# Row gathers of a DLRM tower: each waits for the one before to land, and POOL's program is written out block by block

## What is computed

```
e = stack([tbl_f[ids[:, f]] for f in range(26)], axis=1)      # 2048 x 26 x 64
x = layer_norm(dense @ Wd.T)                                   # 128 values
y = layer_norm(einsum('bnd,ed->bne', e, Ws))
y = layer_norm(einsum('bne,pn->bep', y, Wsi))                  # 32 vectors of 128
T = concatenate([x, y]);  Z = T @ T.T;  z = layer_norm(tril(Z) @ Wl.T) * mask
h = relu([z, dense] @ W1 + b1);  h = relu(h @ W2 + b2);  out = h @ W3
```

## Time and profile before

| | us |
|---|---|
| median of 3 runs | 1114.89 |
| lowest and highest run | 1108.34, 1116.1 |
| span of the profiled execution | 1104.1 |
| of it PE busy | 727.6 |
| of it DVE busy | 468.6 |
| of it POOL busy | 406.8 |
| of it ACT busy | 374.8 |

### The profile page before, as it was taken

The page is one execution under the profiler, slowest core; times in us unless marked ns, Lnnn a source line. Parts: engine busy times, 40 slices in busy tenths (PEclk is TensorE's granted clock), DMA queues, the critical chain, the costliest instruction groups (busy, mean ns, idle before and its releaser), DMA issues.

```text
span 1104.1 us, 18935 instructions
## 1 busy us (share of the span) xinstructions
PE 727.6 (66%) x7419; PEld 555.6 (50%) x7419; DVE 468.6 (42%) x777; ACT 374.8 (34%) x1024; POOL 406.8 (37%) x454
## 2 busy tenths in 40 slices
PE   2226556676666776666786675876666866669977
PEld 1114344454444565545565554564444655448866
DVE  4314245554343445324354342445323454337851
ACT  0022324333332244223243332334323244226742
POOL 6744444424344432344432344423344332440000
PEclk9867666878677877777878777888668877789999
DMA  7300001011101101020110201101110010101110
GB/s 236 110 18 17 15 17 32 14 34 27 29 17 27 31 23 27 13 42 17 27 27 10 40 17 34 23 11 38 24 33 17 13 38 20 33 16 18 28 19 1
DMA packets 30751, 33.94 MB, mean 31 GB/s; under 512 B 10056, under 2 KB 23120, under 8 KB 30288
## 3 DMA queue, kind: packets, MB, share of 16 engines
q1 hardware_dynamic: 17344, 19.08, 7.5%
q0 software_dynamic: 13312, 13.66, 6.4%
q10 hardware_dynamic: 16, 0.01, 0.0%
HBM read 25.37 MB, written 0.01 MB: 23 GB/s over the span
## 4 chain that ended last, share of the span: by engine, by line
another core or an unknown queue 38%; PE 33%; ACT 11%; issue 9%; DVE 7%; SPq 1%; DMA 1%; ACTq 0%; DVEq 0%
PE bank_u L372 13%; ACT emb L704 4%; ACT sq L600 3%; PE bank_g L359 2%; PE bank_t L349 2%; PE bank_z L396 2%; PE bank_y L383 1%; PE bank_m L434 1%; PE bank_y L384 1%; PE bank_y L385 1%; PE bank_h L407 1%; PE bank_m L436 1%; PE bank_m L435 1%; PE bank_h L409 1%
## 5 line engine op out<-in xcount | busy, mean ns | idle before, releaser
L265 POOL DMA_INDIRECT emb<-in_tables,idx x416 | 399.2, 960 | 128.6 <-issue 128.6
L372 PE MATMUL bank_u<-mix_w,emb 128*64 128x192 f32 (+4 forms) x1024 | 159.9, 365 | 70.2 <-ACT emb L704 63.6
L905 DVE RECIPROCAL srs<-sstd 128x32 f32<-128x32 f32 x64 | 22.3, 349 | 427.7 <-ACT sstd L604 387.4
L372 PEld LDWEIGHTS bank_u<-mix_w,emb 128*64 128x64 f32 x1024 | 123.1, 171 | 105.5 <-ACT emb L704 68.4
L247 POOL COPY idx<-ids 128x13 int32 (+1 forms) x33 | 7.3, 222 | 451.5 <-PE bank_u L372 448.1
L589 ACT COPY zc<-bank_z 128x272 f32<-128x272 f32 x64 | 24.4, 381 | 426.7 <-remote 406.0
L396 PE MATMUL bank_z<-tt 128*32 128x34 f32 x4096 | 87.1, 203 | 73.3 <-issue 68.7
L349 PE MATMUL bank_t<-eye,emb 128*128 128x128 f32 x224 | 46.4, 323 | 113.2 <-ACT xb L676 57.2
L396 PEld LDWEIGHTS bank_z<-tt 128*32 128x32 f32 x4096 | 62.4, 112 | 94.9 <-issue 84.6
L704 ACT ACTIVATE emb<-emb,rstd 128x64 f32<-128x64 f32 x416 | 106.3, 339 | 0.0
L359 PE MATMUL bank_g<-gram_w,embt 128*128 128x128 f32 (+1 forms) x448 | 74.7, 314 | 42.7 <-issue 38.3
(11 more groups left out here) (133 smaller groups left out, 1152.5 us busy)
## 6 DMA issues: line engine op xcount, KB each, us to landing
emb<-in_tables,idx POOLq DMA_INDIRECT x416
zs<-zc SPq DMA_DIRECT2D x64, 70.0 KB, 2.4
zs<-zc SPq DMA_DIRECT2D x64, 42.0 KB, 2.1
wfull<-in_wfull SPq DMA_DIRECT2D x1, 2048.0 KB
dtx<-in_dense_pos SPq DMA_DIRECT2D x8, 256.0 KB
dt_f<-in_dense SPq DMA_DIRECT2D x8, 256.0 KB
wz_f<-in_wrows SPq DMA_DIRECT2D x1, 1792.0 KB
wfull<-in_w SPq DMA_DIRECT2D x1, 1280.0 KB
```

The source lines that it names most:

```text
L265: pool.indirect_dma_start(emb[:, k, D * t:D * t + D], None, x_in["tables"], bass.IndirectOffsetOnAxis(ap=idx[:, k, t:t + 1], axis=0),).the ...
L372: mm = pe.matmul(bank_u[D * a:D * a + D, o:o + PR * cnt], emb[:, k, D * t:D * t + D], mix_w[:, t, :, :].rearrange("p s v -> p (s v)")[:, w ...
```

## The change

POOL no longer uses `over_supers`. Its 32 blocks are written out with constants (`gather(n)` for n from 0 to 31). The waits ahead of a block are the same. In front of each gather but the very first there is a new wait: for the landing of the gather before it, by the semaphore on which that one counts (`first_in[k]` for tiles 1 to 8, `rows_in[k]` for tiles 9 to 12, and `rows_in` of the block before for tile 0). Nothing on the other engines changes.

```diff
-            def body(i, blocks, supers):
-                for k in range(4):
-                    n = 4 * i + k
-                    if not blocks(n):
-                        continue
-                    after(pool, mixed, 2 * n - 6)
-                    if blocks(n - 3):
-                        before = i if k < 3 else i + 1
-                        pool.wait_ge(first_in[(k + 1) % 4], 16 * FIRST * before)
-                        pool.wait_ge(rows_in[(k + 1) % 4], 16 * (TILES - FIRST) * before)
-                    pool.wait_ge(idx_ok, n + 1)
-                    if blocks(n + 1):
-                        copy_indices(n + 1, (k + 1) % 4)
-                    for t in range(TILES):
-                        pool.indirect_dma_start(
...
+            def gather(n):
+                k, before = n % 4, (n - 3) // 4 + 1
+                after(pool, mixed, 2 * n - 6)
+                if n >= 3:
+                    pool.wait_ge(first_in[(k + 1) % 4], 16 * FIRST * before)
+                    pool.wait_ge(rows_in[(k + 1) % 4], 16 * (TILES - FIRST) * before)
+                pool.wait_ge(idx_ok, n + 1)
+                if n + 1 < NBLK:
+                    copy_indices(n + 1, (k + 1) % 4)
+                for t in range(TILES):
+                    if 0 < t <= FIRST:
+                        pool.wait_ge(first_in[k], 16 * (FIRST * (n // 4) + t))
+                    elif t:
+                        pool.wait_ge(rows_in[k], 16 * ((TILES - FIRST) * (n // 4) + t - FIRST))
+                    elif n:
+                        pool.wait_ge(rows_in[(k - 1) % 4], 16 * (TILES - FIRST) * ((n - 1) // 4 + 1))
+                    pool.indirect_dma_start(
...
-            over_supers(pool, body)
+            for n in range(NBLK):
+                gather(n)
```

More of the change, by code:

```diff
@@ L247, in copy_indices @@
                 pool.tensor_copy(idx[:, k, :], ids[:, bass.ds(TILES * n, TILES)]).then_inc(idx_ok, 1)
-            def body(i, blocks, supers):
-                for k in range(4):
-                    n = 4 * i + k
-                    if not blocks(n):
-                        continue
-                    after(pool, mixed, 2 * n - 6)
-                    if blocks(n - 3):
-                        before = i if k < 3 else i + 1
-                        pool.wait_ge(first_in[(k + 1) % 4], 16 * FIRST * before)
-                        pool.wait_ge(rows_in[(k + 1) % 4], 16 * (TILES - FIRST) * before)
-                    pool.wait_ge(idx_ok, n + 1)
-                    if blocks(n + 1):
-                        copy_indices(n + 1, (k + 1) % 4)
-                    for t in range(TILES):
-                        pool.indirect_dma_start(
-                            emb[:, k, D * t:D * t + D], None, x_in["tables"],
-                            bass.IndirectOffsetOnAxis(ap=idx[:, k, t:t + 1], axis=0),
-                        ).then_inc(first_in[k] if t < FIRST else rows_in[k], 16)
+            def gather(n):
[15 more added lines that the diff above has]
+                    pool.indirect_dma_start(
+                        emb[:, k, D * t:D * t + D], None, x_in["tables"],
+                        bass.IndirectOffsetOnAxis(ap=idx[:, k, t:t + 1], axis=0),
+                    ).then_inc(first_in[k] if t < FIRST else rows_in[k], 16)
             pool.memset(ids[:, NBLK * TILES:], 0).then_inc(ids_ok, 1)
```

## The result

The changed kernel takes 1287.6 us (median of 4 runs, 1283.3 to 1293.2) beside 1111.6 us for the kernel before: ratio 1.158, 95% interval 1.152 to 1.165. The profiled execution took 1293.2 us with a span of 1291.4: 1.8 us lie around the span, and 1.75 to 1.96 us in every run here that has both numbers, not the 10.8 us that stand ahead of the prediction. The forecast was 1067 us.

A forecast was written before the change was run, and what follows sets the result against it. Bound by waits: ACT for PE's products, POOL for a mix. First gather 4.8, chain 956.8, start 10, long gathers 6.5, tail 77.8, around the span 10.8: 1067 us; range 1007 to 1290.

The forecast's parts named there:

- the link of the chain: POOL's time from one gather's start to the next: 2.30 us, in a chain of 416 gathers, 956.8 us.
- From start to landing, 2.08: A gather's rows are in 2.08 us after its start, read from the trace's byte window of a step's last gather.
- From landing to the next start, 0.22: POOL's release after a landing, taken between idle times of 0.15 and 0.30 us ahead of indirect DMAs; ends 0.10 and 0.30.
- Long links: Gathers long by themselves were to add 6.5 us to the chain, and late landings during the weights' loads 10 us.
- the tail: From the last transposes to the end, second half of step 31 and the drain: 77.8 us.
- break-even: The cost of a gather at which the gain is gone: 2.416 us, a release of 0.34 us.
- rival (b): Each wait ahead of a gather costs more than 0.30 us; with 0.48 a gather takes 2.56, total 1175 us; chance 0.13.
- rival (a): PE's results stay held, now in both halves of a step: slower, 1290 to near 1500 us; chance 0.25.
- the hold: Some 14.7 us between PE's products ending and ACT being told, during POOL's gathers, in 27 steps; forecast to go.
- the one broken beat: One gather took 1.47 us instead of 0.94 and ACT went on 4.2 us later; so pauses may free PE's results.
- POOL sets the pace from first to last: With PE's results freed, POOL's gathers form one chain of 416 that sets the time, 29.9 us a block.
- I take nothing: Writing POOL's program out: register work of 0.33 us in 20 blocks, 7 us if all counted, and instruction fetches, 0 to 5 us.

The follow-up runs named there:

- e6: The changed kernel with all its waits, but 4 wide matmuls instead of the 64 small ones in a products group: 1256.5 us, ratio 1.131 to before.
- e1: The changed kernel's written-out POOL program without any of the new waits: 1085.2 us, ratio 0.973 to the kernel before.
- e7: No waits for landings; POOL writes 800 zeros per partition between any two gathers, a pause of 0.95 us: 907.6 us, ratio 0.816 to before.
- e14: The same kernel as e1, written out without the new waits, on chip 0: 1089.9 us, ratio 0.948 to before.
- e12: The kernel before, unchanged, run for its profile on chip 0: 1144.7 us, ratio 1.000.
- e16: No waits for landings; POOL writes 512 zeros per partition between any two gathers, a pause of 0.71 us, on chip 4: 806.7 us, ratio 0.705 to before.
- e17: The kernel before, unchanged, run for its profile on chip 4: 1144.7 us.
- e2: Each gather waits for the landing of the gather before last, so two are in flight, instead of one in the changed kernel: 869.3 us, ratio 0.774 to before.
- e3: Gathers go out in groups of 4, 4 and 5 a block, each group waiting for all gathers ahead to land: 862.0 us, ratio 0.764 to before.
- e4: No waits for landings; POOL writes 256 zeros per partition between any two gathers, a pause of 0.49 us: 952.4 us, ratio 0.852 to before.

## Why the prediction was wrong, step by step

**The step that failed is the link of the chain,** "Thus a gather costs 2.08 + 0.22 = 2.30 us, with ends of 2.18 and 2.38". It measured 2.90 on average. Its parts:

- *From start to landing, 2.08.* The bytes were through after a median of 2.15: nearly right. But the window showed bytes, and the wait is for the count of the semaphore, which comes 0.33 us later. The forecast took the end of the bytes for the landing. Of everything this costs the most, 0.40 x 416 = 166 us. The earlier trace rows is right as a reading of bytes; it can't show a landing. The Trainium skill's figure (2.0 us plus bytes over 436 GB/s, in "DMA: Bandwidth & Descriptors", "Anatomy of one DMA — SWDGE (gpsimd) path") matched the window by chance: it speaks of the whole time up to the semaphore, and that measured 2.5 us here, not 2.08. Nor does its split hold here, where most of the fixed cost is to lie behind the last byte: of the 2.48 us 1.66 lie ahead of the first packet and 0.33 behind the last.
- *From landing to the next start, 0.22.* Measured 0.26; 0.04 x 416 = 17 us.
- *Long links.* The forecast carried over 6.5 us for gathers that are long by themselves, and 10 for the start. In a chain any delay of a link adds up: the mean is 0.16 above the median of 2.74, 68 us in all. The first block has some 14 of them (its 12 links took 46.5 us). Behind it 23 us are gathers whose descriptors took longer to write (418.0 us busy, against 399.2 before), 11 are longer stretches of packets, 12 are late counts and 6 later starts. What makes them long isn't shown, and how much of it is PE's small matmuls is told under e6.

So the three terms are 0.40 + 0.04 + 0.16 = 0.60 us a link. Against the forecast of 1067 it adds up like this: the chain with its start and its long links was put at 973.3 us and took 1207.8 - 4.8 + 2.4 = 1205.4, thus 232 more; the tail was 3 more; 9 less lie around the span than taken; and the profiled execution was 5.6 longer than the median. 232 + 3 - 9 - 6 = 220 us, and 1287.6 - 1067 is 221.

The sum with the measured link: 4.8 + 415 x 2.90 + 2.4 for the last landing + 81 = 1292 us, the span. The form of the sum was right, then, and so was the point at which it turns: it named 2.416 us a gather as break-even, and a median of 2.74 is past it. The bounds were too narrow: 2.18 to 2.38 treated only the release as unknown, and rival (b), which is what happened and had a chance of 0.13, was sized at 2.56, by a longer release, where it was the landing that was longer. That 1287.6 us lies inside the wide range of 1007 to 1290 is luck: its upper end was put there for rival (a), a hold that stays, and the hold went.

**Right: the hold goes.** The forecast gave 0.25 to a hold that stays and fills both halves of the step. ACT's wait fell from 406.0 to 49.2 us with a longest of 2.5. The argument from the one broken beat came out, and the 11 steps with a long gather in e1 bear it out. e7 shows that the empty queue isn't what does it; whether it is the pause or the rate of the gathers is open.

**Right: POOL sets the pace from first to last,** with the index copy and the loop's register work hidden, and a start-up loss (14 us against 10) and a tail (81.1 against 77.8) near what was taken.

**Wrong, and small beside the rest:** "I take nothing" for writing the program out. Alone it gains 2.7% (e1), on another chip 5.2% (e14). In the trace it is the hold that is shorter in sum, 335 us instead of 406, in the steps with a long gather. In the changed kernel, which has no hold, it should gain nothing; the waits without the writing out weren't run.

**What the price of the whole was.** On one chip (e12 to e14): before 1144.9, written out 1089.9, with the waits 1277.5. The waits take out a hold of some 15 us a block and put in 13 links of 2.90: 37.7 us for a block that had taken 33. With the pause alone (e16) nearly all of the hold goes for 13 x 1.66 = 22 us a block.

## What to carry to other kernels

Before a chain of transfers is costed, read the time until the waiting engine goes on, not until the bytes are through, and take a mean with its long links: a pipeline hides them, a chain adds each one up. If serialising is meant to relieve something else, find out which part of it gives the relief; here a pause of 0.7 us did, at 0.705 of the time of before, where the wait for landing came to 1.158. When a stall has no releaser in the profile, count whether the semaphore's records are all there, and repeat the comparison on another chip before building on it.

## What was not expected of the hardware

- Semaphore updates behind PE's work can be recorded up to 14.6 us after the record of its last matmul ends (15.4 us in e12 and e17) while POOL issues indirect DMAs 0.30 us apart, and the waiting engine starts only then. With pauses of 0.49, 0.71 and 0.95 us the waits ahead of the products' copy fall to 254, 108 and 50 us. What in the chip, or in the recording, does this no run shows.
- It depends on the chip: 656.7 us on one, 1105 to 1151 in every run elsewhere, on at least four others, for the same program. What sets that chip apart is open; before's profile from it is missing.
- One gather that takes over 1.2 us instead of 0.94 comes with a hold of about half the length (5.9 against 12.1 us in e1).
- With the waits, the count of a gather's semaphore is complete 0.33 us after its last packet, in the median, and the waiting indirect DMA starts 0.26 us after that.
- The fastest kernel of this study on a chip with the hold is e16, 806.7 us, whose only addition to the computation is the zeros written to a scratch tile. On the chip without it, the kernel before is the fastest that was run; e1, e2, e3, e4 and e7 weren't run there.
